# Parts of two products put behind the turned keys, affine ahead of a table load, and the last two groups interleaved

## The reference, cut to what matters

```
for d in range(6):
    q, k, v = split(shift(z) @ Wqkv[d])             # 16 heads of 64
    q, k = rotary(l2norm(q)), rotary(l2norm(k))
    z += (softmax(8 q k' + band) v) @ Wo[d]         # the row product
    h = layernorm(shift(z)) * g + b
    z += (h @ W1a + b1a) * gelu(h @ W1g + b1g) @ W2 + b2   # the output product
```

## Time and profile before

| what | us |
|---|---|
| median of 3 runs | 2477.01 |
| lowest, highest | 2473.96, 2479.35 |
| the profiled execution | 2479.06 |
| its span, first to last instruction | 2477.3 |
| TensorE busy | 2364.8 (95%) |
| VectorE busy | 1911.1 (77%) |
| ScalarE busy | 1454.1 (59%) |
| GpSimd busy | 1185.9 (48%) |
| mean of a norm reduction on VectorE (L986, 192 times) | 1.208 |

### The profile page before, as it was taken

One profiled execution on the slowest core, in us unless ns is written; L12 is line 12 of the kernel. 1 busy time (PEld: TensorE's weight loads), 2 busy tenths in 40 slices (PEclk: granted clock), 3 DMA queues, 4 the chain that ended last, 5 costly groups with the idle time before them and its releaser, 6 DMA issues.

```text
span 2477.3 us, 60785 instructions
## 1 busy us (share of the span) xinstructions
PE 2364.8 (95%) x25500; PEld 1430.0 (58%) x25500; DVE 1911.1 (77%) x3471; ACT 1454.1 (59%) x2047; POOL 1185.9 (48%) x883
## 2 busy tenths in 40 slices
PE   6998999999999999999999999978899999999999
PEld 5785656666666666666666666644555555455443
DVE  5889899999999899999999999846866666445222
ACT  2344666666666666666666666634466677566443
POOL 2326777777777777777777777722211111101000
PEclk9999999999999999999999999989899999999999
DMA  4000000000000000000000100002010100120110
GB/s 126 8 7 6 2 2 27 10 8 7 27 10 8 7 27 10 13 2 27 10 13 2 36 2 11 2 1 86 9 38 9 41 28 20 46 87 17 38 54 23
DMA packets 36164, 56.27 MB, mean 23 GB/s; under 512 B 6380, under 2 KB 20852, under 8 KB 35640
## 3 DMA queue, kind: packets, MB, share of 16 engines
q1 hardware_dynamic: 35896, 52.40, 6.8%
HBM read 51.19 MB, written 1.19 MB: 21 GB/s over the span
## 4 chain that ended last, share of the span: by engine, by line
PE 56%; DVE 27%; ACT 12%; issue 5%; POOL 1%; SPq 0%; DMA 0%; DVEq 0%; ACTq 0%
PE w L1392 9%; PE w L1382 9%; DVE turned L979 5%; DVE norm L986 4%; PE w L644 4%; PE w L625 4%; PE w L635 4%; PE py L659 3%; PE w L414 3%; DVE top L430 3%; DVE straight_odd L974 2%; PE w L712 2%; ACT sq L878 2%; PE w L1513 2%; ACT sq L869 2%
## 5 line engine op out<-in xcount | busy, mean ns | idle before, releaser
L425 ACT ACTIVATE prob<-logit 128x512 f32<-128x512 f32 x224 | 137.6, 630 | 278.8 <-DVE logit L433 278.8
L1382 PE MATMUL w<-qT,m_fc 128*128 128x512 f32 x544 | 267.8, 605 | 0.4 <-ACT turned L1631 0.4
L1129 POOL TENSOR_TENSOR straight_odd<-straight_odd,turned 128x1024 f32<-128x1024 f32 x96 | 227.3, 2369 | 82.9 <-DVE turned L979 80.1
L455 POOL TENSOR_TENSOR prob<-prob,rden 128x1024 f32<-128x1024 f32 x112 | 213.5, 1906 | 68.4 <-DVE rden L444 68.4
L979 DVE TENSOR_TENSOR turned<-w,rot 128x512 f32<-128x512 f32 x384 | 245.3, 680 | 0.0
L1129 POOL TENSOR_TENSOR straight<-straight,turned 128x1024 f32<-128x1024 f32 x96 | 226.5, 2369 | 37.3 <-DVE turned L979 37.3
L1123 POOL TENSOR_TENSOR straight_odd<-straight_odd,rnorms 128x1024 f32<-128x1024 f32 x96 | 180.5, 1902 | 115.8 <-DVE rnorms L1000 115.8
L986 DVE TENSOR_REDUCE norm<-sq 128x16 f32<-128x1024 f32 x192 | 224.1, 1208 | 0.0
L1123 POOL TENSOR_TENSOR straight<-straight,rnorms 128x1024 f32<-128x1024 f32 x96 | 180.4, 1899 | 70.0 <-DVE rnorms L1000 70.0
L474 POOL TENSOR_TENSOR fresh_roots<-fresh_means,eps 128x1 f32<-128x1 f32 x64 | 12.1, 190 | 379.1 <-DVE fresh_means L462 379.1
L891 ACT COPY qT<-w 128x1024 f32<-128x1024 f32 x96 | 97.3, 1013 | 162.4 <-PE w L671 162.4
(11 more groups left out here) (253 smaller groups left out, 5295.9 us busy)
## 6 DMA issues: line engine op xcount, KB each, us to landing
b_wqkv<-gates SPq DMA_DIRECT2D x64, 256.0 KB, 3.7
b_wqkv<-in_b_wqkv SPq DMA_DIRECT2D x18, 512.0 KB, 3.5
ctxT<-in_ctxT SPq DMA_DIRECT2D x64, 64.0 KB, 1.8
b_wo<-in_b_wo SPq DMA_DIRECT2D x6, 512.0 KB, 3.5
m_fc<-in_m_fc SPq DMA_DIRECT2D x1, 2304.0 KB, 9.4
m_proj<-in_m_proj SPq DMA_DIRECT2D x1, 2304.0 KB, 13.0
m_fc<-in_m_fc SPq DMA_DIRECT2D x8, 256.0 KB, 3.4
m_proj<-in_m_proj SPq DMA_DIRECT2D x8, 256.0 KB, 3.4
```

What stands on the lines that cost most here:

```text
L455: pool.tensor_tensor(flat, flat, k.rden[:, s, :, None].broadcast_to([P, HEADS, SEQ]), ALU.mult).then_inc(k.prob_ready, 1)
L1129: pool.tensor_tensor(k.straights[s][:, i, :, :], k.straights[s][:, i, :, :], k.turned[:, i, :, :], ALU.add).then_inc(added, 1)
L1382: pe.matmul(claim(("hidden", J, c)), k.m_fc[:, x, c * P:(c + 1) * P], k.m_xT[:, q, :], start=True, stop=True).then_inc(k.ring_full, 1)
```

## The change

On TensorE, six of the eight matmul pairs of the row product stay where they were and the last two are issued behind the turned keys, ahead of the attention product; of the output product's three chunks the third goes to the same place. On ScalarE, affine is put ahead of the table load and the first gelu ahead of the copy of the values. On VectorE, statistics and normalisation of a group are put ahead of the additions of the products. The last group gets banks and buffers of its own (`w1` for `pt` and `py`; parts of `xs`, `kT`, `qT`, `v2`), reads its rows at step 99 beside the hidden step of group 22, has its hidden step at 100 and its output at 102; the loop ends at 102. The four turned outputs use two banks in turn.

```
+AFTER = 2
+LAST_STEP = 6
+LAST_QUAD = {TURN: 3, NORMALISE: 3, HIDDEN: 4, OUTPUT: 6}
 def quad_at(g, lag):
+    if g == STEPS + LAST_QUAD[lag]:
+        return ALL_QUADS - 1
     Q, r = divmod(g - lag, 4)
-    return Q if not r and 0 <= Q < ALL_QUADS else None
+    return Q if not r and 0 <= Q < ALL_QUADS - 1 else None
+def line_bank(k, Q):
+    return k.w1[:, 512:1024] if Q == ALL_QUADS - 1 else k.py[:, :]
+def gate_bank(k, Q):
+    return k.w1[:, 0:512] if Q == ALL_QUADS - 1 else k.pt[:, :]
+def quad_buffers(k, Q):
+    return (k.xs2, k.xnT2, k.gate2, k.hid2) if Q == ALL_QUADS - 1 else (k.xs[:, 0, :, :], k.xnT, k.gate, k.hid)
+def back_bank(k, q):
+    return (k.w0, k.w2)[q % 2]
...
@@ rows, TensorE
-        for h in range(PAIRS):
+        row_heads(p, range(PAIRS - AFTER))
+    def rows_end(p):
+        row_heads(p, range(PAIRS - AFTER, PAIRS)).then_inc(k.row_psum, 1)
...
@@ quad_in
-        if Q:
+        if Q == ALL_QUADS - 1:
+            pe.wait_ge(k.shifted, FIRST + STEPS)
+        elif Q:
             pe.wait_ge(k.gated, 3 * Q)
...
@@ output
+        for c in range(2):
+            output_chunk(Q, c)
+    def output_end(Q):
+        output_chunk(Q, 2).then_inc(k.out_psum, 1)
...
@@ the loop of TensorE
             turn_keys(g - 1, this)
+        if p is not None:
+            rows_end(p)
+        if out is not None:
+            output_end(out)
...
@@ the loop of ScalarE
         if hid is not None:
+            affine(hid)
             act.preload_act_table_set("gelu_and_others")
-            affine(hid)
         if this and not is_cross(g):
             ...
             act.activation(k.sq[:, 1, :, :], k.w1[:, :], ACT.Square).then_inc(k.k_squared, 1)
+        if hid is not None:
+            gelu(hid, 0)
         if before:
             act.wait_ge(k.v_psum, T)
             act.copy(k.v2[:, 1 - s, :, :], k.w2[:, :]).then_inc(k.v_ready, 1)
...
-        if hid is not None:
-            gelu(hid, 0)
...
@@ the loop of VectorE
+        if g == STEPS + LAST_QUAD[TURN]:
+            dve.wait_ge(k.o_psum, FIRST + STEPS)
+            dve.memset(k.hid2[64:P, 2, :], 1.0)
+            quad_stats(ALL_QUADS - 1)
         if hid is not None:
             gate(hid, 0)
+        if g == STEPS + LAST_QUAD[TURN]:
+            quad_normalise(ALL_QUADS - 1)
...
             gate(hid, 2)
+        if quad_at(g, TURN) is not None and g < STEPS + LAST_QUAD[TURN]:
+            quad_stats(quad_at(g, TURN))
+        if quad_at(g, NORMALISE) is not None and g < STEPS + LAST_QUAD[TURN]:
+            quad_normalise(quad_at(g, NORMALISE))
         if p is not None:
             dve.wait_ge(k.row_psum, p + 1)
-            feed(4 * p % (2 * TILES), 4).then_inc(k.row_added, 1)
+            feed(k.py, 4 * p % (2 * TILES), 4).then_inc(k.row_added, 1)
         if out is not None:
             dve.wait_ge(k.out_psum, out + 1)
-            feed(8 * out % (2 * TILES), 8).then_inc(k.z_fed, 1)
-        if quad_at(g, TURN) is not None:
-            quad_stats(quad_at(g, TURN))
-        if quad_at(g, NORMALISE) is not None:
-            quad_normalise(quad_at(g, NORMALISE))
+            feed(line_bank(k, out), 8 * out % (2 * TILES), 8).then_inc(k.z_fed, 1)
```

More of the change, by code:

```diff
@@ L180, in build @@
         k.s_k8 = wide(k.straight).rearrange("p (s j n) -> p s j n", s=2, j=8)
+        k.xs2 = k.xs[:, 1, :, :]
+        k.xnT2 = k.kT[:, :, :, :].rearrange("p a h n -> p (a h n)")[:, 0:512]
+        k.gate2 = k.qT[:, :, :, :].rearrange("p a h n -> p (a h n)")[:, 0:1536].rearrange("p (c n) -> p c n", c=3)
+        k.hid2 = k.v2[:, :, :, :].rearrange("p a b n -> p (a b n)")[:, 0:1536].rearrange("p (c n) -> p c n", c=3)
         k.f_int, k.f_mag = (wide(k.sq)[:, i * P:(i + 1) * P].bitcast(mybir.dt.int32) for i in range(2))
@@ L657, in rows, with row_heads @@
         pe.wait_ge(k.z_fed, quads_before(g, OUTPUT))
-        for h in range(PAIRS):
+        row_heads(p, range(PAIRS - AFTER))
+    def rows_end(p):
+        row_heads(p, range(PAIRS - AFTER, PAIRS)).then_inc(k.row_psum, 1)
+    def row_heads(p, heads):
+        for h in heads:
             mm = pe.matmul(k.py[:, 0:2 * P], k.b_wo[:, h, :], k.oT[:, h, :, :].rearrange("p a n -> p (a n)"),
                            start=(h == 0), stop=(h == PAIRS - 1))
-        mm.then_inc(k.row_psum, 1)
+        return mm
     def turn_queries(g, more):
@@ L723, in quad_in @@
         for j in range(4):
-            mm = pe.transpose(k.pt[:, j * P:(j + 1) * P], shifted_rows(k, (4 * Q + j) % TILES), k.ident[:, :])
+            mm = pe.transpose(gate_bank(k, Q)[:, j * P:(j + 1) * P], shifted_rows(k, (4 * Q + j) % TILES), k.ident[:, :])
         mm.then_inc(k.quad_rows, 1)
@@ L729, in quad_turn @@
         for j in range(4):
-            mm = pe.transpose(k.pt[:, j * P:(j + 1) * P], k.xs[:, 0, j, :], k.ident[:, :])
+            mm = pe.transpose(gate_bank(k, Q)[:, j * P:(j + 1) * P], quad_buffers(k, Q)[0][:, j, :], k.ident[:, :])
         mm.then_inc(k.quad_cols, 1)
@@ L734, in hidden @@
         at, n = CHUNKS[c]
+        xnT = quad_buffers(k, Q)[1]
         if c == 0:
@@ L738, in hidden @@
             pe.wait_ge(k.row_added, pairs_before(g))
-            pe.wait_ge(k.z_fed, quads_before(g, OUTPUT))
+            if Q < ALL_QUADS - 1:
+                pe.wait_ge(k.z_fed, quads_before(g, OUTPUT))
         else:
             pe.wait_ge(k.gated, 3 * Q + c)
-        pe.matmul(k.pt[0:n, :], k.c_w1[:, HID + at:HID + at + n], k.xnT[:, :], start=True,
+        pe.matmul(gate_bank(k, Q)[0:n, :], k.c_w1[:, HID + at:HID + at + n], xnT[:, :], start=True,
                   stop=True).then_inc(k.gate_psum, 1)
@@ L745, in hidden @@
             pe.wait_ge(k.hid_ready, 3 * Q + c)
-        pe.matmul(k.py[0:n, :], k.c_w1[:, at:at + n], k.xnT[:, :], start=True, stop=True).then_inc(k.line_psum, 1)
+        pe.matmul(line_bank(k, Q)[0:n, :], k.c_w1[:, at:at + n], xnT[:, :], start=True, stop=True).then_inc(k.line_psum, 1)
     def output(Q, g):
@@ L750, in output, with output_chunk @@
         pe.wait_ge(k.row_added, pairs_before(g))
[L751 to L754, removed]
+        for c in range(2):
+            output_chunk(Q, c)
+    def output_end(Q):
+        output_chunk(Q, 2).then_inc(k.out_psum, 1)
+    def output_chunk(Q, c):
+        n = CHUNKS[c][1] + (c == 2)
+        return pe.matmul(line_bank(k, Q), k.c_w2[0:n, c, :], quad_buffers(k, Q)[3][0:n, c, :], start=(c == 0), stop=(c == 2))
     def turn_out(q):
-        w = (k.w0, k.w1, k.w2, k.w0)[q]
+        w = back_bank(k, q)
         pe.wait_ge(k.unshifted, q + 1)
-        if q == 3:
-            pe.wait_ge(k.back_added, 1)
+        if q > 1:
+            pe.wait_ge(k.back_added, q - 1)
         for j in range(4):
@@ L769, in layers_tensor @@
     pe.wait_ge(k.loaded, 16 * N_URGENT)
-    for g in range(-TILES, STEPS + OUTPUT + 1):
+    for g in range(-TILES, STEPS + LAST_STEP + 1):
         this, before, before2 = stages_of(g)
@@ L838, in affine @@
         act.wait_ge(k.c_loaded, 48 * (Q // QUADS + 1))
-        act.activation(k.xnT[:, :], k.pt[:, :], ACT.Identity, bias=k.c_cols[:, 1:2],
+        act.activation(quad_buffers(k, Q)[1][:, :], gate_bank(k, Q), ACT.Identity, bias=k.c_cols[:, 1:2],
                        scale=k.c_cols[:, 0:1]).then_inc(k.xn_ready, 1)
@@ L844, in gelu @@
         act.wait_ge(k.gate_psum, 3 * Q + c + 1)
-        act.activation(k.gate[0:n, c, :], k.pt[0:n, :], ACT.Gelu, bias=k.c_cols[0:n, 5 + c:6 + c]).then_inc(k.gated, 1)
+        act.activation(quad_buffers(k, Q)[2][0:n, c, :], gate_bank(k, Q)[0:n, :], ACT.Gelu, bias=k.c_cols[0:n, 5 + c:6 + c]).then_inc(k.gated, 1)
     def unshift(q):
@@ L1001, in refine_norms, with feed @@
                                  op1=ALU.mult).then_inc(k.newton_step, 1)
-    def feed(first, n):
-        cols = k.py[:, 0:n * SEQ].rearrange("p (b n) -> p b n", n=SEQ)
+    def feed(bank, first, n):
+        cols = bank[:, 0:n * SEQ].rearrange("p (b n) -> p b n", n=SEQ)
         low, high = k.z[0:64, first:first + n, :], k.z[64:P, first:first + n, 1:SEQ]
@@ L1014, in quad_stats @@
         for j in range(4):
-            last = dve.bn_stats(k.stats4[:, j, :], k.pt[:, j * P:(j + 1) * P])
+            last = dve.bn_stats(k.stats4[:, j, :], gate_bank(k, Q)[:, j * P:(j + 1) * P])
         last.then_inc(k.quad_stat, 1)
@@ L1024, in quad_normalise @@
         for j in range(4):
-            last = dve.tensor_scalar(k.xs[:, 0, j, :], k.pt[:, j * P:(j + 1) * P], k.mv4[:, j, 0:1],
+            last = dve.tensor_scalar(quad_buffers(k, Q)[0][:, j, :], gate_bank(k, Q)[:, j * P:(j + 1) * P], k.mv4[:, j, 0:1],
                                      k.rstd4[:, j:j + 1], ALU.subtract, ALU.mult)
@@ L1032, in gate @@
         dve.wait_ge(k.gated, 3 * Q + c + 1)
-        dve.scalar_tensor_tensor(out=k.hid[0:n, c, :], in0=k.py[0:n, :], scalar=k.c_cols[0:n, 2 + c:3 + c],
-                                 in1=k.gate[0:n, c, :], op0=ALU.add, op1=ALU.mult).then_inc(k.hid_ready, 1)
```

(4 more changed lines are left out.)

## The result

| | us |
|---|---|
| changed kernel, median of 4 | 2442.48 (2442.37 to 2444.71) |
| before, median of 4 | 2475.49 (2472.88 to 2479.35) |
| ratio, 95% interval | 0.9868 (0.985 to 0.9885) |
| span of the profiled execution | 2440.7 (before 2477.3) |

Faster by 1.3%, at the time forecast. First the stretches of one period, cut at the query products as in the earlier trace rows; the columns are the stretch, its length in us, the busy time of PE, PEld, DVE, ACT and POOL, the granted clock, the DMA share and GB/s.

What follows compares the result with a forecast made beforehand. TensorE and VectorE were taken as both nearly full in three steps of four. Terms 19.4 + 6.6 + 0.9 + 9.3 = 36.2 us off 2479.06 gave 2442.9, stated as 2442, range 2428 to 2457.

Steps and rivals of the forecast that it cites:

- Part 1, the split: Row and output steps: moved product pieces cover the attention product's wait for ScalarE's copy; 0.30 us a period, 6.6 in all.
- The wait of the turned keys in the output step: Output step: turned keys, with room of 0.65 us against 0.87 of move and 0.44 gained, would wait for VectorE's key rotation.
- I take VectorE's 0.3: Row, output and row steps together: gain set at VectorE's 0.3 us a period, between bounds of 0 and 1.32.
- Rival B: Local stage: VectorE takes nothing from the split, its own work filling three steps; 2449 us, period 58.8, chance 0.17.
- Part 2: Hidden step: ScalarE's new order starts VectorE's first gate earlier; 0.88 us in each of 22 hidden steps, 19.4 in all.
- rival E: Hidden step: affine under the exponential set needs an extra table load of 1.28 us, 28 in all; 2470 us, chance 0.04.
- Part 3, the tail: Last two groups: earlier turns and interleaving 6.6 us, clock 2.7; 9.3 in all, from 6.6 to 11.4.
- the clock's part: Last two groups: with TensorE's idle spots before the two turns gone, full clock saves 2.7 us, bounds 0 and 4.8.
- rival C: Local stage: VectorE never limits, 22 x 1.02 us more gained; 2420 us, period 57.5, chance 0.10 including halfway cases.
- rival F: Local stage: turns start no earlier, moved parts delay the attention product, 70 steps lose 0.43 us; 2483, period 60.1, chance 0.04.
- Rival D: Tail: the clock stays low there, the rest as forecast; 2445 us, chance 0.12.
- the late end of the row product: Row step: product ends 2.6 us later at no cost, covered by VectorE's norm reductions, statistics and normalisation; 0.2 if uncovered.

Runs made afterwards that it cites:

- the tail alone: The kernel before with the last two groups interleaved, VectorE's new order only from step 96, products whole, ScalarE's old order: 2465.7 us against 2476.8.
- the split alone: The kernel before with both products split behind the turned keys and VectorE's new order up to step 95, nothing else: 2474.7 us against 2476.8.

## Why the prediction was right, and where only by luck

The time came out within 1 us, but two terms were mis-sized and made up for each other: in the traces the stage up to step 95 gave 20.9 (23.0 less the 1.3 and 0.8 of chance) for 26.9 forecast, and the tail 13.6 for 9.3. The starting point helped as well. The sum of 36.2 was taken off an execution of 2479.06; off the median of 2475.49 measured beside the changed kernel it would give 2439.3, and by the medians the gain was 33.0. That the time fell so near the forecast is in part luck.

- Part 1, the split, "22 x 0.30 = 6.6". Measured 0.05 or 0.06 a period together with VectorE's new order, about 1 us. The wait of the turned keys in the output step was foreseen and is there, and there VectorE gains what the forecast said: from one maximum to the next 13.51 for 13.75, 0.24, its wait ahead of the key rotation being gone. What failed is "I take VectorE's 0.3" for the three steps together. The two row steps take VectorE 14.84 for 14.78 and 14.26 for 14.14, so that of the 0.24 only some 0.06 is left (42.61 for 42.67 over the three). The row steps are as long with the products whole (14.84 and 14.25), so that loss comes with VectorE's new order, to which the forecast gave no cost and which costs 0.11 a period. On TensorE a row step gained 0.35, for 0.44, by the 0.09 for a split. Rival B described the stage better than the forecast, though VectorE does take something from the split.
- Part 2, "22 x 0.88 = 19.4". Right in mechanism and size: 0.90 a period alone, 21 us, and VectorE's wait for the first gelu fell from 2.16 to 1.24. That affine's place gives nothing by itself followed from the forecast's chain, and the kernel with the gelu put back shows it. No third table load came (44 in the 22 hidden steps), so rival E is out.
- Part 3, the tail, "9.3, from 6.6 to 11.4". Measured 13.6 in the one pair of traces, above the range; the tail alone gave 11 by the medians, within it. The chain of the last two groups was right (the last gates end 8.1 us apart, 1632.14 and 1640.20; the forecast's 10.9, less its 2.0 for the clock, is 8.9); the clock's part was taken as 2.7 of 4.8 and is 5.0 in the kernel before with fillers. Left out was the last row product: 3.72 instead of 6.09, since the clock was back in time. Without these 2.4 the tail would be 11.2, within the range. The forecast gave no reason for them, and why the clock was back is open, as the split alone shows (6.70).
- The period of 58.69 rules out rival C (57.5) and rival F (60.1). It lies nearer to B's 58.8 than to the forecast's 58.5. Rival D is out too: the clock was 1.00 in the hidden steps of the last two groups.
- VectorE does not wait for the late end of the row product: the statistics and the normalisation cover it, as forecast.

## What to carry to other kernels

A repeated wait of the busiest engine is worth only what the second busiest lets through: cover one and look whether the next step that joins the two engines grows by the same amount. Here the hidden step took back 0.50 of 0.53, 0.11 of it through the new order on VectorE that came with the split. So run a reordering that only makes room for another change by itself, too. Look for the gain where the second engine waits, and move what stands on a third engine between its input and its result. In a stretch that is one chain, count the clock beside the instructions: behind an idle spot of 2.42 us a pair of matmuls took 2.07 for 1.12, and unused matmuls in the spots added no time. Do not count on the same clock in the next kernel: the last row product took 3.72 in one and 6.70 in another behind the same instructions.

## What the hardware showed that I had not expected

In the tail the granted clock fell to 0.50, that is from 2.4 to 1.2 GHz, in or right behind idle spots of 2.4 to 4.4 us, and groups at the low clock took 1.97 for 1.09 (eight transposes) and 6.09 for 3.72 (the last row product). With unused matmuls in these spots it was 1.00 there. The Trainium skill, TensorE: Matmul & The Clock Gate, "Part 1: The HAM clock gate (the "warmup" mystery)", has these two rates and says they follow how busy the engine has been; the traces agree. And a group of matmuls cut in two cost 0.09 us more than in one piece, in row and output steps alike.
